# Main attention of a two-layer transformer kernel: where preparation, sums, output products and row maxima stand in the written-out order

## The reference, cut to what matters

```python
qf = concat([q_nope, apply_rope(q_pe)])          # 128 + 64 wide
kf = concat([k_nope, apply_rope(k_pe)])
scores = einsum('bhqd,bhkd->bhqk', qf, kf) * 192 ** -0.5
probs = softmax(scores)
ctx = einsum('bhqk,bhkd->bhqd', probs, v)
main_out = ctx.reshape(...) @ o_w.T
return gates[..., 0:1] * main_out + gates[..., 1:2] * pattern_out
```

## Time and profile before

| | |
|---|---|
| Median of three runs | 1562.99 us |
| The profiled execution: time, span | 1566.81 us, 1565.0 us |
| Main attention (first to last score tile) | about 311 to 909 us of the span |
| PE busy, whole span | 91% |
| DVE, ACT, POOL busy, whole span | 59%, 48%, 35% |

### The profile page before, as it was taken

How to read it: one execution, slowest core, us unless ns; L and a number is a source line. 1 busy time by engine, 2 the same in 40 slices (tenths; PEclk the granted TensorE clock), 3 DMA queues, 4 the chain that set the end, 5 groups by cost and what they waited for, 6 DMA issues and landing times. The chain is left out here.

```text
span 1565.0 us, 20565 instructions
## 1 busy us (share of the span) xinstructions
PE 1426.5 (91%) x7287; PEld 841.9 (54%) x7350; DVE 926.7 (59%) x1719; ACT 747.3 (48%) x1368; POOL 548.9 (35%) x454
## 2 busy tenths in 40 slices
PE   6889999899999999999999968899579999879998
PEld 3533333355455555454545546788434444468887
DVE  5588776456666666666666344444458787544445
ACT  3457776654545454545453324233235555435553
POOL 4260162155565655656566522233200000101210
PEclk9979999999999999999999968899789999959999
DMA  7980000000000000000001011110076000101110
GB/s 292 179 114 1 2 21 7 1 1 0 1 1 0 1 1 1 1 1 1 1 1 42 0 41 39 36 55 27 1 168 93 1 1 1 50 21 41 41 41 27
DMA packets 20442, 53.04 MB, mean 34 GB/s; under 512 B 4630, under 2 KB 7464, under 8 KB 19123
## 3 DMA queue, kind: packets, MB, share of 16 engines
q1 hardware_dynamic: 20341, 51.73, 13.6%
HBM read 42.28 MB, written 8.39 MB: 32 GB/s over the span
## 5 line engine op out<-in xcount | busy, mean ns | idle before, releaser
L1631 POOL TENSOR_TENSOR Ps<-Ps,Pb 128x512 f32<-128x512 f32 x192 | 245.3, 1291 | 161.4 <-ACT Pb L1614 161.4
L1614 ACT ACTIVATE Pb<-bank 128x512 f32<-128x512 f32 x256 | 152.9, 597 | 287.5 <-PE bank L1603 235.0
L1575 DVE TENSOR_REDUCE mp<-bank 128x1 f32<-128x512 f32 x256 | 171.7, 687 | 141.6 <-PE bank L1568 139.7
L1062 DVE TENSOR_REDUCE mp<-bank 128x2 f32<-128x1024 f32 x128 | 153.6, 1222 | 48.4 <-PE bank L1054 48.0
L1121 ACT ACTIVATE Pb<-bank 128x512 f32<-128x512 f32 x256 | 133.2, 600 | 39.7 <-PE bank L1104 39.3
L1568 PE MATMUL bank<-qk1h,qk0h 128*128 128x512 f32 x256 | 135.7, 541 | 7.7 <-DVE mp L1575 7.7
L1600 PE MATMUL bank<-qk0h,qk1h 128*128 128x512 f32 x256 | 124.3, 486 | 6.1 <-DVE mrow L996 6.1
L1645 PE MATMUL bank<-Pb,kvx 128*64 128x512 f32 x512 | 124.0, 605 | 1.0 <-ACT Pb L1614 0.7
L1246 ACT ACTIVATE Pb<-bank 128x512 f32<-128x512 f32 x192 | 84.7, 489 | 80.2 <-PE bank L1233 57.4
L1214 DVE TENSOR_REDUCE mp<-bank 128x1 f32<-128x512 f32 (+1 forms) x192 | 97.8, 552 | 17.6 <-PE bank L1204 11.5
L1602 PE MATMUL bank<-qk0h,qk1l 128*128 128x512 f32 x256 | 101.2, 396 | 0.0
(11 more groups left out here) (341 smaller groups left out, 3265.5 us busy)
## 6 DMA issues: line engine op xcount, KB each, us to landing
wr<-wf SPq DMA_DIRECT2D x25, 256.0 KB, 2.6
wraw<-wf SPq DMA_DIRECT2D x8, 768.0 KB, 4.1
scratch<-stgr SPq DMA_DIRECT2D x4, 1024.0 KB, 3.9
scratch<-stg SPq DMA_DIRECT2D x4, 768.0 KB, 7.0
owT<-owT SPq DMA_DIRECT2D x1, 2048.0 KB, 9.9
qbn<-qbn SPq DMA_DIRECT2D x1, 1536.0 KB, 14.9
qstr<-scratch SPq DMA_DIRECT2D x12, 128.0 KB
kstr<-scratch SPq DMA_DIRECT2D x12, 128.0 KB
```

The lines of the kernel that those rows point to most:

```text
L1062: e.tensor_reduce(mp[:, w % 3, :, j, kh], wide[slot][:], AX, ALU.max).then_inc(ring_ok, 1)
L1575: e.tensor_reduce(mp[:, u % 3, hd, j, kh:kh + 1], bank[b][:, 0:c], AX, ALU.max).then_inc(mp_ok[2], 1)
L1614: e.activation(Pbm[n % NPBM][:], bank[b][:], ACT.Exp, scale=SC0).then_inc(exp_ok[2], 1)
L1631: e.tensor_tensor(Ps[z][:], first, Pbm[n % NPBM][:], ALU.add).then_inc(sum_ok, 1)
```

## The change

The prep steps get a fixed time t each: t = 16 * (u % 2) + k. Each part's product is placed after tile 1, 5, 9, 13, 17 or 21, and each further step of the part one tile later, so that a low part and the next part's product fall on the same tile. The steps `den` and both parts of `project` move so that they stand directly before a `pv`. `neg`, `tr` and `row` come earlier in the unit. The maxima are spread over tiles 0 (even units) or 2 (odd units) to 9. `ctx` and `cadd` get fixed tiles of their own. Counts and shapes of all instructions stay.

```diff
-        begin, last_max = (0, nk) if ahead == 2 else (3 * (u % 2), nk - 5)
+        begin, last_max = (0, nk) if ahead == 2 else (2 * (u % 2), nk - 6)
...
-PREP_TIMES = (0, 1, 2, None, 3, 4, 5, None, 6, 7, 8, None, 9, 10, 11, None, 12, 13, 14, None, 15, 16, 17, None, 18, 19)
+R0, R1, R2, R3, Q0, Q1 = ("rope", 0), ("rope", 1), ("rope", 2), ("rope", 3), ("lat", 0), ("lat", 1)
+PRODUCT_AT = ((R0, 1), (Q0, 5), (R1, 9), (R2, 13), (Q1, 17), (R3, 21))
+AFTER = {"rope": ("product", "swap", "turn", "high", "low"), "lat": ("product", "high", "low")}
+PREP = [tuple((part, AFTER[part[0]][t - at]) for part, at in PRODUCT_AT if 0 <= t - at < len(AFTER[part[0]]))
+        for t in range(32)]
...
-    chunks = []
-    out = [(kind, i) for i in range(NT) for kind in ("ctx", "cadd")]
+    out = {u: {k + d: (("ctx", "cadd")[d], 4 * u + i) for i, k in enumerate(ks) for d in range(2)}
+           for u, ks in ((0, (0, 4, 8, 10)), (1, (0, 2, 4, 6)))}
...
-        if u % 2 == 0 and u // 2 + 1 < 8:
-            chunks.extend(("prep", u // 2 + 1, i) if i is not None else None for i in PREP_TIMES)
...
-        now = [c for c in chunks[:1] if chunks.pop(0) is not None]
-        if (u == 0 and 1 <= k < 13) or (u == 1 and 2 <= k < 6):
-            now.append(out.pop(0))
+        now, t = [], 16 * (u % 2) + k
+        if u // 2 + 1 < 8 and PREP[t]:
+            now.append(("prep", u // 2 + 1, t))
+        if k in out.get(u, ()):
+            now.append(out[u][k])
...
-        return [(0, [("den", u)]), (1, [("recip", u)]), (4, [("project", u, 0)]), (6, [("project", u, 1)])]
-    order = attention_order(16, 2, False, 2, 1, (2, 3, -4, -2), at_begin, at_step, evac, lead=False)
+        return [(1, [("den", u)]), (2, [("recip", u)]), (5, [("project", u, 0)]), (9, [("project", u, 1)])]
+    order = attention_order(16, 2, False, 2, 1, (2, 3, -5, -4), at_begin, at_step, evac, lead=False)
...
-PREP = (
-    ((R0, "product"),), ((R0, "swap"),), ((R0, "turn"),),
-    ((R0, "high"), (Q0, "product")), ((R0, "low"), (Q0, "high")), ((Q0, "low"),),
...
-    ((R3, "product"),), ((R3, "swap"),), ((R3, "turn"),), ((R3, "high"),), ((R3, "low"),),
-)
```

More of the change, by code:

```diff
@@ L215, in causal_order @@
     return attention_order(32, 1, True, 4, 2, (2, 2, 0, 2), lambda u: [], at_step, lambda u: [(0, [("evac", u)])])
-R0, R1, R2, R3, Q0, Q1 = ("rope", 0), ("rope", 1), ("rope", 2), ("rope", 3), ("lat", 0), ("lat", 1)
-PREP = (
-    ((R0, "product"),), ((R0, "swap"),), ((R0, "turn"),),
-    ((R0, "high"), (Q0, "product")), ((R0, "low"), (Q0, "high")), ((Q0, "low"),),
-    ((R1, "product"),), ((R1, "swap"),), ((R1, "turn"),),
-    ((R1, "high"), (R2, "product")), ((R2, "swap"), (R1, "low")), ((R2, "turn"),),
-    ((R2, "high"), (Q1, "product")), ((Q1, "high"), (R2, "low")), ((Q1, "low"),),
-    ((R3, "product"),), ((R3, "swap"),), ((R3, "turn"),), ((R3, "high"),), ((R3, "low"),),
-)
 FIRST = (R0, R1, R2, Q0, Q1, R3)
```

## The result

The changed kernel took 1653.2 us (median of four executions, 1645.07 to 1656.36) against 1563.75 for the kernel before (1559.78 to 1569.35): ratio 1.0561, 95% interval 1.0511 to 1.0612. The forecast was 1626 us with a range from 1580 to 1645. The direction and the places were right; the loss is 89.5 us where I had worked out 63, outside the range.

What follows compares the result with a forecast made beforehand. PE bounds the stage. New gaps of 13.6 us less 3.0 of old gaps and 0.8 of shapes give +9.8 a pair: +59 for six middle pairs, +5 first, -1 last, together +63: 1626 us, range 1580 to 1645.

Steps and rivals of the forecast that it cites:

- R0, R1, R2 held by the swap: At three rotated prep parts, score tiles on PE wait for an exponential behind ACT's swap: 1.0, 1.9, 2.1 us a pair.
- R3's stretch: At the fourth rotated part, DVE's turn waits for the swap and delays a maximum's reduction: 1.8 us a pair lost.
- maxima behind R2's high and low part: Unit 4's maxima on PE wait because their first reduction stands behind the late low part on DVE: 1.6 us lost.
- Q1's low part: On DVE it stands between two reductions, maxima in close pairs; the maximum before 3.1.2 waits 1.8 us.
- transposes behind low, additions, `neg`: After R3, DVE's low part, four additions and `neg` end at T+14.0; PE reaches the transposes at 12.05: 2.0 lost.
- second `project` behind the rows: In odd units it comes one tile after the transposes and waits for the rows to leave bank 6: 0.7 lost.
- joined shapes, and `den`: `project` directly before `pv` saves 0.2 us on PE, four times a pair, 0.8 in all; `den` saves nothing.
- S0: The score tile between a `pv` and the moved swap; S1, S2, S3 are the tiles after it.
- T: The moment when S0 is through on PE, from which the forecast counts times.
- the clock falls: Rival: gaps lower PE's busy share and granted clock to 0.95, products grow by about 30 us: 1655 us, chance 0.06.
- only ACT's order: Rival: the chain over POOL and DVE is absorbed, +2.8 us a pair remains: 1581 us, chance 0.21.
- faster: Rival: ACT's 2.4 us swap is absorbed, S3 isn't held, 1.3 us a pair won: 1552 us or so, chance 0.09.

Runs made afterwards that it cites:

- swap_early: The changed kernel with each swap directly behind its product, before the next exponential on ACT: 1606.44 us, ratio 1.0251.
- small_sums: The changed kernel with POOL's additions cut to eight columns from key block 2 on: 1613.25 us, one execution.
- ctx_first: The changed kernel with `ctx` and `cadd` ahead of the prep step of the same tile: 1644.74 us, one execution.
- rows_under_pv: The kernel before with `tr` and `row` one tile earlier, directly ahead of the `pv` after tile 13: 1564.45 us, ratio 1.0001.
- swap_rows: swap_early with `neg`, `tr` and `row` where the kernel before had them: 1607.12 us, one execution.
- joined_only: The kernel before with only the new places of `den`, `recip` and `project`: 1576.92 us, ratio 1.0086.
- chain_rows: chain_early with `neg`, `tr` and `row` where the kernel before had them: 1588.3 us, ratio 1.0156.
- chain_early: The changed kernel with each swap directly behind its product, and turn, high and low parts one tile earlier: 1589.96 us, ratio 1.0142.
- rows_late: The changed kernel with `neg`, `tr` and `row` where the kernel before had them: 1627.59 us, ratio 1.0388.
- prep_only: The kernel before with only the new times of the prep steps: 1591.66 us, ratio 1.0170.

## Why the prediction was wrong in size

By its own terms, the first middle pair (what PE lost in the profile of the changed kernel, by distances between starts). This pair is itself 12.0 us longer than before; the mean of the six is 12.3, as four of them lose more by the clock:

| Term | forecast | measured |
|---|---|---|
| R0, R1, R2 held by the swap | 1.0, 1.9, 2.1 | 1.0, 1.9, 2.2 |
| R3's stretch | 1.8 | 1.7 |
| maxima behind R2's high and low part | 1.6 | 1.3 |
| Q1's low part | 1.8 | 1.7 |
| Q0's low part | 0.7 | 1.3 |
| transposes behind low, additions, `neg` | 2.0 | 3.2 |
| second `project` behind the rows | 0.7 | 2.0 to 2.2 |
| joined shapes, and `den` | -0.8 | -1.0 |
| old gaps gone | -3.0 | -3.4 |
| sum | +9.8 | +12.0 |

- **Held tiles: right.** The step "exponential of S0 from T+0.2 to 0.8, swap to 3.2" came out to the tenth, and swap_early shows that it is the cause. Behind R2, 0.6 of the 1.3 us is PE waiting for the high part itself: the forecast had both times, PE there at T+8.7 and the high part over at T+9.2, and counted no wait.
- **The transposes: mis-sized.** The failed step is "low part on DVE to 10.8 (two of 0.69, up to 0.9 beside POOL)" and "`neg` (1.6, most of it the 1.2 of L985)". Measured: low over at T+11.5, `neg` 2.1. I priced the low part by one row without POOL beside it. By line, the same operations averaged 1.59 and 1.18 for keys in the two middle pairs of the kernel before (0.87 and 0.68 for queries, which R3 is), so the dear form was in the trace. And the 1.2 of L985 for eight columns was a warning that I took for a price: it is 0.17 alone.
- **The clock: put at nothing.** "In odd units lost 0.7" was right for the row wait itself (0.53 idle). The rest of the 2.0 to 2.2 there is the clock, 0.7 at `project` and 0.9 at `pv`. "Against: my gaps are 2 us at most" was the argument with which I set the falling clock aside. It failed twice: the gap at the transposes grew to 3, and in two of six pairs the clock also fell behind R2's 1.78, a gap of the size that I had forecast. The one middle pair of ctx_first without a fall takes 86.8 us, at a clock of 1.00, where the others take 87.9 to 88.9. By that the clock costs the changed kernel 1.6 us in a pair at 0.98 (88.4) and 2.0 in one at 0.96 (88.8). That is an estimate of 11 us for six pairs, out of 74.
- **The rival "the clock falls"** had the nearest time, 1655 us, and part of the mechanism. Middle pairs were granted 0.96 to 0.98, not 0.95, and it costs some 11 us there, not 30, since it falls for short stretches behind single waits and some of it is taken up by waits that shrink. Its time is near by luck: what it left out, the waits themselves, is the larger part.
- **The rival "only ACT's order"** (1581) is refuted by swap_early and small_sums: shortening POOL's sums takes off 40 of the 89.5 us.
- **The rival "faster"** needed the exponential of S1 over by T+1.9. It starts at T+3.2 (478.88 in ACT's rows).
- **Ends.** Last pair -0.6, forecast -1: right. First pair +17.7, forecast +5: the failed step is "loses a wait for `ctx` of about 2: I take +5". I had counted `ctx` as a gain and not gone through ACT's list there, where the copy of `ctx` now stands behind high parts. ctx_first shows 10.5 of the 17.7.
- **Joined shapes: right**, 0.20 each; `den`, costed at nothing, saves 0.1. With the missing 2.5 a pair (15 us, most of it the clock's) and 12.7 of the first pair the forecast would have stood at 1654. Its own unknowns at their dearest, 6 and 10 us, gave only 1642.

No complete kernel tried is faster than the one before; the nearest, rows_under_pv, is the same.

## What to carry to other kernels

Price a step on DVE by the form it has beside its new neighbours: look for a line's second duration, since an eight-column operation of 1.2 us is a wait, not a cost. When steps in a fixed order are moved together, follow each engine's list to the last waiter, also in the odd first round, and add up waits that fall on one instruction. Give the clock a term of its own: here a fall cost about 1.6 us, and waits of 1.4 to 3.1 us had one behind them in some pairs and none in others. Steps that share a bank (here `project` and the rows) have to be moved as one.

## What the runs showed of the hardware

- **DVE stands still while POOL adds.** The subtraction of eight columns took 1.18 us beside POOL's sums and 0.17 without, the cast 0.71 and 0.17, a low operation from `Rt` 1.68 and 0.68. POOL lost too: one of its sums took 1.69 beside the end of such an operation, the next 1.25. Reductions from a bank (686 ns, and 688 in small_sums), L1704 and the low parts that read a bank (694 and 695 ns) didn't change. The Trainium skill, "SBUF — State Buffer", "Who interferes with whom", says that a DVE instruction with two inputs in SBUF, or one in a two-port mode such as a cast can enter, contends with a GpSimd instruction that reads SBUF, that the later one blocks until the other ends, and that a DVE instruction with at most one such input doesn't. All these rows agree with it. The forecast had not used it.
- **The clock.** Behind some waits of PE the products ran at 1.2 GHz for a time, behind others at 2.4, and the length of the single wait doesn't decide which. In the six middle pairs the clock fell behind the wait at the transposes of 3.04 us in six (changed kernel), of 3.04 in five (ctx_first), of 2.76 in six (swap_rows), of 2.26 in two (joined_only), of 1.54 in three (chain_rows) and of 1.41 in one (swap_early, chain_early). Behind R1's hold of 1.84 it fell in six (rows_late), behind R2's of 1.78 in two (changed kernel) and in none (small_sums). One fall made a pair 1.6 us longer in prep_only, swap_early and chain_rows, and 0.8 to 1.2 in joined_only. The Trainium skill, "TensorE: Matmul & The Clock Gate", Part 1, calls the slow clock the default that activity lifts; the windows of 0.96 to 0.98 and 0.93 here, with more idle time than before, are in line with that.
- **Shapes.** `project` directly before `pv` saves 0.20 us, `den` before `pv` 0.11. Both came out the same in every kernel that has them.
